# First attention in 64x64 tiles without the masked quarter: a hybrid layer kernel on one core

## The reference

```
x = x + attn_a(layernorm(x))      # linear attention, 16 heads of 64, causal
x = x + ffn(layernorm(x))         # int8-quantised 512x512 product
x = x + attn_b(layernorm(x))      # decayed state of 16x32 for 16 heads, RoPE, gate, its own layer norm
x = x + ffn(layernorm(x))
```

```
k_cumsum = cumsum(k);  context = cumsum(outer(k, v))     # over the sequence
D_inv    = 1 / (k_cumsum . q)
attn     = (q @ context) * D_inv                         # then @ Wo + bo
```

## Time and profile before

| | |
|---|---|
| median of 3 runs | 3187.48 us (3184.71 to 3187.89) |
| the profiled execution's own time | 3186.5 us |
| span of its profile | 3184.8 us |
| busy: TensorE matmul / weight load | 3066.7 us (96%) / 2322.5 us (73%) |
| busy: VectorE / ScalarE / GpSimd | 2141.9 us (67%) / 644.4 us (20%) / 1013.7 us (32%) |
| mean granted TensorE clock | 0.988 of 2.4 GHz |

### The profile page before, as it was taken

The page is one execution under the profiler, slowest core; times in us unless marked ns, Lnnn a source line. Parts: engine busy times, 40 slices in busy tenths (PEclk is TensorE's granted clock), DMA queues, the critical chain, the costliest instruction groups (busy, mean ns, idle before and its releaser), DMA issues.

```text
span 3184.8 us, 104441 instructions
## 1 busy us (share of the span) xinstructions
PE 3066.7 (96%) x44692; PEld 2322.5 (73%) x44692; DVE 2141.9 (67%) x4764; ACT 644.4 (20%) x1165; POOL 1013.7 (32%) x1394
## 2 busy tenths in 40 slices
PE   3699999999999999999999999999999999999995
PEld 2577777777777777777777777777777777777764
DVE  6766666666666666666666667667667667667665
ACT  2121121121121122122122122122122112112111
POOL 2023333333333333333333333333333333333333
PEclk9899999999999999999999999999999999999998
DMA  5222221222222222222222222222222222222121
GB/s 174 62 44 43 43 50 42 43 50 42 43 49 44 44 46 46 45 45 43 47 44 43 46 44 43 47 44 46 44 44 46 43 44 47 45 43 46 45 39 26
DMA packets 384299, 152.36 MB, mean 48 GB/s; under 512 B 352800, under 2 KB 361632, under 8 KB 383904
## 3 DMA queue, kind: packets, MB, share of 16 engines
q1 hardware_dynamic: 383904, 146.02, 23.8%
HBM read 45.29 MB, written 16.78 MB: 19 GB/s over the span
## 4 chain that ended last, share of the span: by engine, by line
PE 95%; DVE 3%; DMA 1%; issue 1%; ACT 0%; POOL 0%; SPq 0%; POOLq 0%; DVEq 0%
PE bank L689 22%; PE bank L690 21%; PE bank L691 21%; PE bank L937 7%; PE bank L752 4%; PE bank L778 4%; PE bank L820 3%; PE bank L889 2%; PE bank L647 2%; PE bank L765 2%; PE bank L792 2%; PE bank L912 2%; PE bank L899 1%; PE bank L925 1%; DVE absmax L1069 1%
## 5 line engine op out<-in xcount | busy, mean ns | idle before, releaser
L689 PE MATMUL bank<-xbT,wb 128*128 128x128 f16 x2048 | 350.5, 221 | 17.9 <-DMA xbT<-work 17.9
L689 PE MATMUL bank<-xaT,wq_hi 128*128 128x128 f16 x2048 | 359.9, 221 | 4.0 <-DVE wk_lo L1094 4.0
L609 POOL TENSOR_TENSOR work<-work 128x512 f32<-128x512 f32 x128 | 200.1, 1564 | 500.1 <-DVE work L1316 500.1
L691 PE MATMUL bank<-xaT,wq_lo 128*128 128x128 f16 x2048 | 358.6, 220 | 0.0
L690 PE MATMUL bank<-xaT,wq_hi 128*128 128x128 f16 x2048 | 358.5, 220 | 0.0
L689 PE MATMUL bank<-xaT,wk_hi 128*128 128x128 f16 x2048 | 358.2, 220 | 0.0
L691 PE MATMUL bank<-xaT,wk_lo 128*128 128x128 f16 x2048 | 358.1, 220 | 0.0
L690 PE MATMUL bank<-xaT,wk_hi 128*128 128x128 f16 x2048 | 358.1, 220 | 0.0
L690 PE MATMUL bank<-xbT,wb 128*128 128x128 f16 x2048 | 350.5, 221 | 0.0
L691 PE MATMUL bank<-xbT,wb 128*128 128x128 f16 x2048 | 350.4, 221 | 0.0
L1349 DVE TENSOR_TENSOR work<-bank,causal 128x512 f32<-128x512 f32 x256 | 159.0, 683 | 186.0 <-PE bank L889 186.0
(11 more groups left out here) (202 smaller groups left out, 8081.4 us busy)
## 6 DMA issues: line engine op xcount, KB each, us to landing
xin<-in_L_attn_a_x SPq DMA_DIRECT2D x64, 256.0 KB, 2.6
out<-xf SPq DMA_DIRECT2D x64, 256.0 KB, 2.0
table<-in_tables SPq DMA_DIRECT2D x64, 192.5 KB, 2.9
work<-in_L_attn_a_Wq SPq DMA_DIRECT2D x1, 2048.0 KB, 9.1
work<-in_L_attn_a_Wk SPq DMA_DIRECT2D x1, 2048.0 KB, 14.8
wb<-in_L_attn_a_Wv SPq DMA_DIRECT2D x1, 2048.0 KB, 19.4
work<-in_L_attn_a_Wo SPq DMA_DIRECT2D x1, 2048.0 KB, 8.5
work<-work SPq DMA_TRANSPOSE x128, 3.1
```

Source lines behind the costliest of these rows:

```text
L609: pool.tensor_tensor(to[:, :, :, :], to[:, :, :, :], cross[:, :, ::-1, :], ALU.add)\
L689: nc.tensor.matmul(o, a[0], b[0], start=first, stop=False)
L691: return nc.tensor.matmul(o, a[1], b[0], start=False, stop=last)
```

## The change

Scores and score times v are computed in 64x64 tiles. Of the four tiles (half of the keys, half of the queries) of a pair the one with later keys and earlier queries is all masked, and it is no longer computed. So that the three remaining tiles of a pair use the array's four quarters evenly, the halves are swapped for some heads: `key_half(pair, place)` says which half of the keys lies at which partition half (swapped for odd pairs), `query_half(pair, place)` the same for the queries of the output (swapped for pairs 2, 3, 6, 7).

- `s(g)` has 24 matmuls of 64x64 tiles with 64 columns moving in place of 8 of 64x128 with 128. Its bank quarter that isn't computed keeps an old number, which the mask sets to zero; all banks of scores are cleared once at the start.
- `o(g)` becomes two steps, `oa` and `ob`, of 12 matmuls each with 64x64 tiles and 65 columns, in place of 16 of 128x64. In the second half each head's product comes from the other row half of the array, so it first waits until the first half's last matmul of that group has finished (`o_half`).
- `so(g)` has the same number of matmuls as before; it takes the banks of `o(g)` itself.
- Before each of `s`, `so`, `oa`, `ob` TensorE's queue gets one instruction of its own, a semaphore increment (`waited`), which carries the last wait.
- `qk_(i)` reads x with swapped halves for k of the odd pair (12 of 48 matmuls); `v(g)` takes the even pairs' columns for g = 0 and the odd pairs' for g = 1, and its eviction `v1_e` becomes two instructions, which write each half of the rows to the other place. Both `v0` and `v1` are now needed by every `o` and `u`.
- `o_e(g)` has three multiplications for each head of a pair instead of one: one for two pairs in place and two for the half partitions of the swapped pairs.
- The mask `causals` holds two masks in f16, 3 more selects on GpSimd at the start.
- A new ORDER (largest lag 5, before 4; with it 12 unrolled first slots, before 10), new BANK, LATE, BORROWED and COUNTS.

The core of the diff:

```diff
+def key_half(pair, place):
+    return place ^ (pair & 1)
+def query_half(pair, place):
+    return place ^ (pair >> 1 & 1)
...
+            def shares(place_k, place_q, heads):
+                return [(m, key_half(m, place_k), q) for m in heads for q in place_q(m)
+                        if q >= key_half(m, place_k)]
+            def waited():
+                pe.sem_inc(small_tiles_begun, 1)
...
             def s(g):
                 def step(c):
                     pair = [c.take(f"s{g}a"), c.take(f"s{g}b")]
-                    c.take(f"o{g}a")
-                    c.take(f"o{g}b")
-                    c.done(f"u{g}", 1)
                     c.done(f"qk{2 * g}")
                     c.done(f"qk{2 * g + 1}")
+                    waited()
+                    heads = range(4 * g, 4 * g + 4)
+                    places = [shares(place, lambda m: (0, 1), heads) for place in range(2)]
+                    for n in range(len(places[0])):
+                        for place in range(2):
+                            m, k, q = places[place][n]
+                            for p, (bank, f) in enumerate(pair):
+                                at = tile(m - 4 * g).start + HALF * q
+                                last = nc.tensor.matmul(bank[half_of(place), at:at + HALF], qk[half_of(p), 1, m, half_of(place)],
+                                                        qk[half_of(p), 0, m, half_of(q)], start=True, stop=True,
+                                                        skip_group_check=True)
...
+            def o(g, half):
+                def step(c):
+                    if half == 0:
+                        c.done("v0")
+                        c.done("v1")
+                        c.done(f"s{g}a")
+                        c.done(f"s{g}b")
+                    else:
+                        c.wait(o_half[g], c.count())
+                    waited()
+                    now = [place ^ half for place in range(2)]
+                    todo = [[shares(place_k, lambda m: (query_half(m, place_q),), range(4 * g, 4 * g + 4))
+                             for place_q in range(2)] for place_k in range(2)]
+                    for j in range(3):
+                        for place_k, p in enumerate(now):
+                            bank, f, _ = c.bank(f"o{g}{'ab'[p]}")
+                            for place_q in range(2):
+                                m, k, q = todo[place_k][place_q][j]
+                                i = m - 4 * g
+                                last = nc.tensor.matmul(bank[half_of(place_q), i * VA:(i + 1) * VA],
+                                                        sc[g][half_of(place_k), p, i, half_of(q)],
+                                                        va[half_of(place_k), 2 * m + p, :], start=False,
+                                                        stop=half == 1 and j == 2, skip_group_check=True)
+                    if half == 0:
+                        last.then_inc(o_half[g], 1)
...
-                        nc.vector.tensor_tensor(attn[:, 4 * g:4 * g + 4, p, :], o4[:, :, 0:DA],
-                                                recip_d[:, g, p, :, None].to_broadcast([P, 4, DA]), ALU.mult).then_inc(e, 1)
+                        nc.vector.tensor_tensor(attn[:, 4 * g:4 * g + 2, p, :], o4[:, 0:2, 0:DA],
+                                                recip_d[:, g, p, 0:2, None].to_broadcast([P, 2, DA]), ALU.mult)
+                        for place in range(2):
+                            h = half_of(place)
+                            last = nc.vector.tensor_tensor(attn[half_of(query_half(2, place)), 4 * g + 2:4 * g + 4, p, :],
+                                                           o4[h, 2:4, 0:DA],
+                                                           recip_d[h, g, p, 2:4, None].to_broadcast([HALF, 2, DA]), ALU.mult)
+                        last.then_inc(e, 1)
...
+            for b in sorted({BANK[u] for u in ("s0a", "s0b", "s1a", "s1b")}):
+                nc.vector.memset(ps[b][:, :], 0.0)
```

More of the change, by code:

```diff
@@ L38 @@
 MAGIC = 1.5 * 2.0 ** 23
-ORDER = [("out_e", 4), ("nb_rs", 3), ("qk2", 1), ("no_st", 4), ("ub_e", 4), ("wo1", 2), ("no_rs", 4), ("no_ap", 4),
[13 rows of a table removed]
-         ("out", 3), ("nb_st", 2)]
+ORDER = [("qr_e", 4), ("xhb", 4), ("sb", 4), ("ys", 4), ("mm1_e", 5), ("sb_e1", 4), ("qk2", 1), ("ub", 4), ("sb_e0", 4),
+         ("mm1_a", 5), ("aT1_l", 2), ("qk1_e", 1), ("yb", 4), ("aT1_t", 2), ("u1", 2), ("y_e", 4), ("u0", 2),
+         ("ub_e", 4), ("ld_t", 3), ("mm0_a", 3), ("u0_e", 2), ("nb_st", 3), ("nb_rs", 3), ("kt0", 1),
+         ("bias", 2), ("u1_e", 2), ("out", 4), ("qk2_e", 1), ("wo0", 2), ("out_e", 4), ("no_st", 4),
+         ("kt0_e", 1), ("wo1", 2), ("no_ap", 4), ("no_rs", 4), ("no_f", 4), ("nb_ap", 3), ("xTb_h", 3),
[4 rows of a table added]
+         ("s1_e", 1), ("gb", 3), ("v1_e", 1), ("kb_e", 3), ("ub_a", 4), ("kb_a", 3), ("qb_e", 3), ("kb_h", 3),
[5 rows of a table added]
 LAG = dict(ORDER)
@@ L60 @@
 MAX_LAG = max(LAG.values())
[L63 to L66, removed]
+BANK = {"v0": 5, "v1": 4, "qk0": 5, "qk1": 2, "qk2": 0, "qk3": 7, "kt0": 4, "s0a": 3, "s0b": 6, "o0a": 0, "o0b": 2,
+        "u0": 3, "kt1": 4, "s1a": 0, "s1b": 2, "o1a": 3, "o1b": 6, "u1": 6, "wo": 1, "mm0": 7, "qb": 7, "kb": 1,
+        "vb": 1, "gb": 5, "qr": 1, "kr": 4, "sb0": 3, "sb1": 4, "sb2": 5, "sb3": 6, "y0": 7, "y1": 1, "ub": 5,
+        "out": 2, "mm1": 0}
 BANKS = 8
-TAKES = {"s0a": "s0", "s0b": "s0", "s1a": "s1", "s1b": "s1", "o0a": "s0", "o0b": "s0", "o1a": "s1", "o1b": "s1",
+TAKES = {"s0a": "s0", "s0b": "s0", "s1a": "s1", "s1b": "s1", "o0a": "so0", "o0b": "so0", "o1a": "so1", "o1b": "so1",
          "wo": "wo0", "y0": "sb", "y1": "sb", "sb0": "sb", "sb1": "sb", "sb2": "sb", "sb3": "sb"}
@@ L84 @@
 LATE = {
[L85 to L98, removed]
[8 rows of a table removed]
+    (0, "qr_e"): ("load o",),
+    (0, "qk0_e"): ("max o", "all o", "turn decay"),
+    (1, "wo_e"): ("scale o", "hi o", "keep decay"),
+    (1, "rnd1"): ("lo o", "load rhs", "load bk"),
+    (1, "ob1"): ("max rhs", "all rhs"),
+    (1, "qk0"): ("columns of rhs", "rows of rhs"),
+    (1, "qT1_t"): ("scale rhs",),
+    (1, "aT0_l"): ("max bk", "all bk"),
+    (2, "qr_e"): ("scale bk", "hi bk"),
+    (2, "u0"): ("round rhs", "load bq"),
+    (2, "nb_rs"): ("lo bk", "load g", "load rk", "load rq"),
+    (2, "no_ap"): ("max bq", "all bq"),
[10 rows of a table added]
 }
 TAKEN = ("q", "k", "v", "o", "rhs", "bk", "bq", "g", "bv", "rk", "rq")
-BORROWED = {"decay": (0, "qk1_e", 0),
-            "o": (0, "qk1_e", 2),
-            "rhs": (1, "s1_e", 3),
-            "rhs rows": (1, "o0_e", 5),
-            "bk": (1, "u0_e", 7),
-            "bq": (2, "wo1", 2),
-            "g": (2, "xTb_l", 1),
-            "bv": (2, "s0_e", 1),
-            "rk": (2, "s1_e", 3),
-            "rq": (2, "o0_e", 5)}
+BORROWED = {"decay": (0, "qk0_e", 1),
+            "o": (0, "qk0_e", 6),
+            "rhs": (1, "ob1", 1),
+            "rhs rows": (1, "qk0", 7),
+            "bk": (1, "aT0_l", 6),
+            "bq": (2, "no_ap", 6),
+            "g": (2, "s0", 2),
+            "bv": (2, "gb", 0),
+            "rk": (2, "ob1", 1),
+            "rq": (2, "qk0", 0)}
 def borrowed_before(bank, slot, place):
@@ L400, in hybrid_kernel @@
         s_pool = sem("pool_step")
+        s_mask = sem("mask_of_swapped_keys")
+        small_tiles_begun = sem("small_tiles_begun")
+        o_half = [sem(f"first_half_of_o{g}") for g in range(2)]
         s_dve = sem("vector_step")
@@ L944, in _ @@
             run(pe, "PE", dict(v0=v(0), v1=v(1), qk0=qk_(0), qk1=qk_(1), qk2=qk_(2), qk3=qk_(3), kt0=kt(0), kt1=kt(1),
-                         s0=s(0), s1=s(1), so0=so(0), so1=so(1), o0=o(0), o1=o(1), u0=u(0), u1=u(1),
+                         s0=s(0), s1=s(1), so0=so(0), so1=so(1), oa0=o(0, 0), ob0=o(0, 1), oa1=o(1, 0), ob1=o(1, 1), u0=u(0), u1=u(1),
                          wo0=wo_(0), wo1=wo_(1), mm0=mm(0), mm1=mm(1),
@@ L977, in step @@
                     bank, e = c.read(f"v{g}")
-                    c.filled(f"o{g}b", 1)
-                    c.filled(f"u{g}", 1)
-                    nc.scalar.activation(va[:, 8 * g:8 * g + 8, 0:DA], bank[:, :].rearrange("p (h e) -> p h e", h=8),
-                                         ACT.Copy).then_inc(e, 1)
+                    for n in ("o0a", "o0b", "o1a", "o1b", "u0", "u1"):
+                        c.filled(n, 1)
+                    to = va[:, :, 0:DA].rearrange("p (m two h) e -> p m two h e", two=2, h=2)[:, :, g, :, :]
+                    rows = bank[:, :].rearrange("p (m h e) -> p m h e", m=4, h=2)
+                    if g == 0:
+                        nc.scalar.activation(to, rows, ACT.Copy).then_inc(e, 1)
+                    else:
+                        for place in range(2):
+                            last = nc.scalar.activation(to[half_of(place)], rows[half_of(key_half(1, place))], ACT.Copy)
+                        last.then_inc(e, 1)
                 return step
```

95 lines of the change are left out of this document (52 added, 43 removed), and 57 rows, old and new, of tables (COUNTS, LATE, ORDER).

## The result

The changed kernel takes 3157.6 us (median of 4 runs, 3157.05 to 3159.74), the kernel before 3187.2 in the same comparison: ratio 0.991 [0.990, 0.992], 29.6 us or 0.9% faster. Forecast were 3127 us; the gain is half of the 60.5 us expected. The time lies inside the range, 30 us above the forecast and 2 us above rival A's 3155.

What follows compares the result with a forecast made beforehand. TensorE's own list was taken as the bound, 47.52 us a slot. Tiles save 1.08 us, markers cost 0.10, net 0.98 over 62 chunks: 61 us off 3187.5, say 3127 us, range 3112 to 3168.

Steps and rivals of the forecast that it cites:

- rival A: TensorE's semaphore increments before s, so, oa, ob aren't covered, up to 0.56 us a slot: 3155 us, chance 0.21.
- Streaming and changes of shape: TensorE's attention steps: 5.34 us a slot with the new tiles against 6.42 before, 1.08 us less.
- Rival C: Tiles of s and o don't go four abreast, 192 records at 0.029 us: +104 us, 3291 us, chance 0.03.
- Markers: The 8 semaphore increments a slot in TensorE's queue, six inside stretches, with their waits: 0.10 us a slot.
- Rival B: Each of six inner increments drains TensorE's array, 0.36 us each, 2.2 us a slot: 3255 us, chance 0.09.
- The order: The new list walked with old durations: no handoff makes TensorE wait; oa1 has some 2 us slack.
- rival D: A handoff is late every slot, likely oa1 behind s1_e; a 1 us stall gives 3187 us, chance 0.05.
- Only the length of TensorE's own list counts: From 320 to 3076.7 us TensorE is always busy, so no wait there is worth anything; 47.52 us a slot.
- VectorE: o_e's multiplications go from 1.68 to 3.26 us a slot, 33.7 us of work in 46.5, hidden.
- Start and end: First slots and final chain of attn_b: taken as 0, bounds -10 to +20 us and within 5 us.

Runs made afterwards that it cites:

- edge_wo1: The changed kernel with its cyclic ORDER begun at wo1, so the loop's edge lies between wo0 and wo1, behind long matmuls; 3147.3 us, ratio 0.988.
- edge_pad64: edge_wo1 with 64 semaphore increments at the start of TensorE's queue; 3138.0 us, ratio 0.985.
- pad128: The changed kernel with 128 semaphore increments at the start of TensorE's queue; 3231.6 us.
- edge_pad212: edge_wo1 with 212 semaphore increments at the start of TensorE's queue; 3213.4 us.
- the cut: vb's 12 matmuls of 512 columns moved between so0 and oa0, in edge_pad64 and in edge_pad212; 3154.3 and 3173.7 us.
- edge_pad88: edge_wo1 with 88 semaphore increments at the start of TensorE's queue; 3144.0 us.
- edge_pad80: edge_wo1 with 80 semaphore increments at the start of TensorE's queue; 3142.4 us.
- edge_pad96: edge_wo1 with 96 semaphore increments at the start of TensorE's queue; 3172.3 us.
- after_pad64: The changed kernel, loop's edge left before sb, with 64 semaphore increments at the start of TensorE's queue; 3250.6 us.

## Why the prediction was wrong

- **Streaming and changes of shape** (1.08 us less a slot): right. The shortest slot is 46.59 us, 0.93 less than before with the markers in it. s0 and s1 1.58 for 1.6, so1 to ob0 2.57 for 2.5; 0.0147 us a record holds inside a step. Rival C, and with it the Trainium skill's floor of 25 ns between starts ("TensorE: Matmul & The Clock Gate", section "Wait — 56ns, not 53.3ns?"), is refuted for four tiles side by side.
- **Markers** 0.10 us a slot: right in size for one each. Rival B (an increment drains the array, 0.36 us) is refuted by the gaps of 0.01 to 0.04 us. Rival A had a time near the measured one (3155) for a reason that isn't there, since single markers are covered; that the time lies in the range, whose upper end was taken from rival A, is luck. The mechanism "small tiles use up a lead of TensorE's queue" was the right thought, though not at the marker: at the block.
- **The order, "none is late by that walk"**: right for what the walk looked at. No handoff between engines is late inside the loop; rival D didn't happen. **This is the step that failed, by what it left out**: it walked data and semaphores and took TensorE's instructions as always there, and it didn't ask where the rotated list puts the loop's edge. "Only the length of TensorE's own list counts" was true of the kernel before, whose fastest block took 3.0 us and whose edge lay behind long matmuls.
- **What it cost**, by the slots: 47.035 - 46.54 = 0.49 us, over 59 slots 29 us. Moving the edge gives back 0.18 (edge_wo1; 0.06 of it is the exit slot), moving the boundaries 0.14 more (edge_pad64), together 0.32 of the 0.49; 0.05 is the 46.59 against 46.54. The last 0.12 are, in edge_pad64, two stalls ahead of the loop (1.8 and 0.6 us, 0.04 a slot) and 0.03 to 0.13 us in nearly every loop slot, most of it in s1 of every second one; that was not taken apart.
- **VectorE**: the multiplications of o_e take 222.5 us over 64 chunks, 3.48 each; the estimate was 12 x 0.272 = 3.26. Hidden all the same. **Start and end** at nothing: right, within 1 us.

Open: what starts a packet's fetch. At the changed kernel's place it starts between 0.6 us before the boundary is passed and 0.2 after; in pad128 0.6 to 1.6 us after it, with stalls of 0.9 to 2.2 us, in edge_pad212 1.1 to 2.0 after, with 1.5 to 2.4. Slow matmuls ahead of the boundary go with the early start, but no run separated the two. Once the packet is under way, its end sets the stall: in the changed kernel's 26 passes it ends at most 0.71 us after the boundary is passed where there is no stall, 0.70 to 0.80 after where there are 0.3 us, and 0.9 to 1.14 after where there are 0.57. A version free of stalls at any placement and without the 0.22 us of the cut was not found.

## What to carry to other kernels

Where a change replaces few long matmuls by many short ones, look at how long the densest 256 instructions last. At 3.0 us nothing stalled here (kernel before), at 3.1 there were 0.3 us in the mean (edge_pad88), at 2.1 to 2.3 up to 2.4 us at some placements and nothing at others; edge_pad80 shows that there is no sharp bound. Time such a change with several paddings ahead of it, since a single time judges the padding too (for the same work here 3138 to 3195 us, the 18 us of edge_pad212's increments taken off its 3213). And put the edge of a hardware loop behind long matmuls, which are still under way while the block behind the jump is fetched.

## What the runs showed of the hardware

- TensorE's program arrives in packets of 16.4 KB, 256 instructions; the loop of 3249 takes 13 or 14 fetches an iteration, the old one of 2852 took 12. From a packet's start to its first instruction 2.2 to 2.9 us where TensorE waited for it inside a step (changed kernel, pad128, edge_pad212, edge_pad96), 3.2 to 3.7 us behind the jump (after_pad64).
- A weight load and a matmul count as two instructions, so 64x64 tiles of f32, four side by side, use up 256 instructions in about 2.1 us; the kernel before needed 3.0 us for its fastest block.
- A semaphore increment on TensorE's sequencer takes 0.151 us, one behind the other (pad128); one is hidden between small matmuls, three are not.
- A jump back, with the loop's register waits behind it, costs sb 0.2 us at a good place (changed kernel) and 2.7 to 3.9 us at a bad one (after_pad64), with 1.2 us of work queued ahead of it. Behind `out` and wo0 it showed no stall at any of the six paddings of edge_wo1.
- After rests of 1.9 to 3.9 us TensorE's granted clock fell to half for 3.4 or 6.8 us, though not after each: once in the changed kernel (loop's exit), 18 times in after_pad64, never inside the loop of the kernel before, which has no rest there.
